# Attention of a graph network on one core: products and additions moved to GpSimd, one softmax for two chunks

## What is computed

```python
Q = (x @ Wq).reshape(N, H, D)      # N = 512, H = 8 heads, D = 32
K = (x @ Wk).reshape(N, H, D)
V = (x @ Wv).reshape(N, H, D)
score = jnp.einsum('nhd,ngd->nhg', Q, K) / np.sqrt(D)
score = jax.nn.softmax(score, axis=-1)
x1 = jnp.einsum('nhg,ngd->nhd', score, V).reshape(N, H * D)
msg = x1[dst] * x1[src]
attn_out = jax.ops.segment_sum(msg, dst, num_segments=N)
```

## Time and profile before

| | us |
|---|---|
| three runs before | 594.47, 595.21, 595.46 (median 595.21) |
| the profiled execution | 594.7 |
| its span | 592.6 |
| busy in it: TensorE, VectorE, ScalarE, GpSimd | 573.7, 462.4, 369.1, 224.1 |
| granted TensorE clock, mean | 0.999 |

### The profile page before, as it was taken

One profiled execution on the slowest core, in us unless ns is written; L12 is line 12 of the kernel. 1 busy time (PEld: TensorE's weight loads), 2 busy tenths in 40 slices (PEclk: granted clock), 3 DMA queues, 4 the chain that ended last, 5 costly groups with the idle time before them and its releaser, 6 DMA issues.

```text
span 592.6 us, 8599 instructions
## 1 busy us (share of the span) xinstructions
PE 573.7 (97%) x3032; PEld 487.7 (82%) x3032; DVE 462.4 (78%) x795; ACT 369.1 (62%) x565; POOL 224.1 (38%) x211
## 2 busy tenths in 40 slices
PE   7989999999999999999999999999999999898895
PEld 6778888888888888888888888888888889577763
DVE  5986497778878887788998789879766566798667
ACT  6866786777777766777766778757275543311242
POOL 4075577556666544554444555430000000000011
PEclk9999999999999999999999999999999999999999
DMA  8255487285576636546553875223182404000000
GB/s 295 79 205 175 143 288 218 106 285 172 170 223 189 215 106 214 160 155 212 178 192 128 319 239 164 91 81 91 46 317 74 152 0 143 0 2 0 1 0 35
DMA packets 34504, 86.86 MB, mean 147 GB/s; under 512 B 3872, under 2 KB 23200, under 8 KB 29856
## 3 DMA queue, kind: packets, MB, share of 16 engines
q1 hardware_dynamic: 27264, 67.09, 36.0%
q0 software_dynamic: 6912, 19.10, 8.5%
q10 hardware_dynamic: 288, 0.13, 0.1%
HBM read 66.69 MB, written 19.62 MB: 146 GB/s over the span
## 4 chain that ended last, share of the span: by engine, by line
PE 83%; DVE 10%; ACT 2%; issue 2%; POOL 1%; DMA 1%; POOLq 0%; DVEq 0%; ACTq 0%
PE ps L1337 27%; PE ps L1389 10%; PE ps L1543 7%; PE ps L1395 5%; PE ps L1371 5%; PE ps L1432 5%; PE ps L1367 4%; PE ps L1366 4%; PE ps L1507 4%; PE ps L1434 2%; PE ps L1585 2%; PE ps L1636 1%; PE ps L1555 1%; PE ps L1574 1%; PE ps L1351 1%
## 5 line engine op out<-in xcount | busy, mean ns | idle before, releaser
L483 POOL DMA_INDIRECT sorted_rows<-m,place x120 | 167.1, 1393 | 151.5 <-ACT m L546 123.5
L529 ACT ACTIVATE m_hi<-ps,cols 128x512 fp32r<-128x512 f32 x128 | 88.6, 692 | 67.0 <-PE ps L1337 41.5
L864 DVE TENSOR_TENSOR m_lo<-m_out,m_hi 128x512 fp32r<-128x512 f32 x128 | 88.5, 693 | 51.2 <-ACT m_out L531 48.2
L1337 PE MATMUL ps<-x_hi,w_hi 128*128 128x512 f32 x248 | 97.0, 391 | 0.5 <-DVE x_lo L738 0.5
L1337 PE MATMUL ps<-x_lo,w_hi 128*128 128x512 f32 x248 | 96.9, 391 | 0.0
L1337 PE MATMUL ps<-x_hi,w_lo 128*128 128x512 f32 x248 | 96.7, 390 | 0.0
L531 ACT ACTIVATE m_out<-ps,cols 128x512 f32<-128x512 f32 x128 | 88.5, 691 | 1.8 <-DVE m_lo L864 1.8
L738 DVE TENSOR_TENSOR x_lo<-x_raw,x_hi 128x1024 fp32r<-128x1024 f32 x62 | 73.1, 1218 | 5.3 <-ACT x_hi L523 5.3
L1389 PE MATMUL ps<-w_lo,m_hi 128*128 128x256 f32 x256 | 64.2, 283 | 0.0
L1389 PE MATMUL ps<-w_hi,m_hi 128*128 128x256 f32 x256 | 64.0, 282 | 0.0
L546 ACT ACTIVATE m<-m_in 128x512 f32<-128x512 f32 x64 | 39.5, 634 | 38.0 <-DVE m_in L877 38.0
(11 more groups left out here) (229 smaller groups left out, 1136.7 us busy)
## 6 DMA issues: line engine op xcount, KB each, us to landing
x_raw<-in_edges_dram SPq DMA_DIRECT2D x31, 1024.0 KB, 6.1
sorted_raw<-sorted_rows SPq DMA_DIRECT2D x24, 647.5 KB, 4.6
sorted_raw<-sorted_rows SPq DMA_DIRECT2D x6, 518.0 KB, 4.0
d_w<-in_d_dram SPq DMA_DIRECT2D x3, 1024.0 KB, 8.7
d_w<-in_d_dram SPq DMA_DIRECT2D x1, 3072.0 KB, 10.4
rows<-in_rows_dram SPq DMA_DIRECT2D x1, 2176.0 KB, 10.2
sorted_rows<-m,place POOLq DMA_INDIRECT x120, 4.8
w_raw<-in_w_dram SPq DMA_DIRECT2D x4, 256.0 KB, 5.4
```

What stands on the lines that cost most here:

```text
L483: pool.indirect_dma_start(out=sorted_d, out_offset=bass.IndirectOffsetOnAxis(ap=place[:, at:at + 1], axis=0), in_=m2[:, b % 2, t], in_offs ...
L529: nc.scalar.activation(out_hi[:, m], ps[:, bank], ACT.Gelu, bias=col(bias, m)).then_inc(hi_signal, 1)
L864: nc.vector.tensor_tensor(lo[:, m], m_out[:, m], hi[:, m].bitcast(F32), ALU.subtract).then_inc(done, 1)
L1337: last = nc.tensor.matmul(out, left, right, start=(k == 0 and i == 0), stop=(k == KE - 1 and i == 2))
```

## The change

The chunks' products are made and added in another split:

- GpSimd gets three instructions: `halves_of(0)` and `halves_of(1)` add the two halves (1024 elements each) of the output products 0 and 1; `last_scores(LOW_HEADS)` makes the half of score product 3 that belongs to heads 0 to 3 (1024 elements). VectorE makes the other half and no longer adds any halves; TensorE sums four parts of chunk 1 instead of eight.
- Score product 0 is made in two pieces of 1024 elements, the first ahead of the wait for the power and the normalized rows, and TensorE sums four parts after each piece.
- `less_top`, `exponential` and `softmax` take a range of chunks; chunks 2 and 3 go through them together, after the score reduction of chunk 3.
- TensorE's order becomes: `qkv(3)`, sum of scores 2, output sums 0 and 1, `gather(0)`, `gather(1)`, output sum 2, `gather(2)`, `gather(3)`. ScalarE's copies and exponentials follow it.

```diff
--- before.py
+++ after.py
@@ -280,6 +280,21 @@
 
             return ps[:, 2 + half, k * NH:(k + 1) * NH]
 
+        def last_scores(heads):
+
+            q = qk_rows[:, 3, 0:H].rearrange("p (h a d) -> p h a d", h=HEADS, a=1)
+            k = qk_rows[:, 3, H:2 * H].rearrange("p (a g d) -> p a g d", a=1, g=HEADS)
+            part = [P, heads.stop - heads.start, HEADS, DH]
+            out = prod[3].rearrange("p (h g d) -> p h g d", h=HEADS, g=HEADS)
+            return out[:, heads], q[:, heads].to_broadcast(part), k.to_broadcast(part), ALU.mult
+
+        LOW_HEADS, HIGH_HEADS = slice(0, HEADS // 2), slice(HEADS // 2, HEADS)
+
+        def halves_of(c):
+
+            half = HEADS * H // 2
+            return prod[c][:, 0:half], prod[c][:, 0:half], prod[c][:, half:], ALU.add
+
         def row_half(r):
 
             return r.rearrange("p (a f) -> p a f", a=1).to_broadcast([P, NC // 2, H])
@@ -330,6 +345,7 @@
         qkv_done, qkv_out = sem("qkv_done"), sem("qkv_out")
         scores_ready, exp_done = sem("scores_ready"), sem("exp_done")
         prod_ready, prod_summed = sem("prod_ready"), sem("prod_summed")
+        out_made, out_halved, scores_half = sem("out_made"), sem("out_halved"), sem("scores_half")
         x1_out, x1_ready, gathered = sem("x1_out"), sem("x1_ready"), sem("gathered")
         rz_weights = sem("rz_weights")
         wqk_ready, wv_ready = sem("wqk_ready"), sem("wv_ready")
@@ -503,6 +519,12 @@
             for half in range(2):
                 inverse_std(NODE_HALF[half])
                 inverse_std(NODE_HALF[half])
+            pool.wait_ge(out_made, 1)
+            pool.tensor_tensor(*halves_of(0)).then_inc(out_halved, 1)
+            pool.wait_ge(qkv_out, 2 * NC)
+            pool.tensor_tensor(*last_scores(LOW_HEADS)).then_inc(scores_half, 1)
+            pool.wait_ge(out_made, 2)
+            pool.tensor_tensor(*halves_of(1)).then_inc(out_halved, 1)
             for _ in ("o", "f2"):
                 for half in range(2):
                     inverse_std(NODE_HALF[half])
@@ -686,9 +708,9 @@
             nc.scalar.activation(wv_turned[:].rearrange("p k (d g) -> p k d g", g=HEADS),
                                  wv[:].rearrange("p k (g d) -> p k d g", g=HEADS), ACT.Copy).then_inc(wv_ready, 1)
 
-            def exponential(c, at):
+            def exponential(c, past, at):
                 act.wait_ge(scores_ready, at)
-                nc.scalar.activation(probs[:, c], probs[:, c], ACT.Exp, scale=float(DH) ** -0.5).then_inc(exp_done, 1)
+                nc.scalar.activation(probs[:, c:past], probs[:, c:past], ACT.Exp, scale=float(DH) ** -0.5).then_inc(exp_done, 1)
 
             def sums_out(c, at):
 
@@ -700,14 +722,13 @@
             qkv(0)
             qkv(1)
             affine(1, None, None)
-            exponential(0, 1)
-            exponential(1, 2)
+            exponential(0, 1, 1)
+            exponential(1, 2, 2)
             qkv(2)
             qkv(3)
-            sums_out(0, 3)
-            exponential(2, 3)
+            sums_out(0, 4)
+            exponential(2, 4, 3)
             sums_out(1, 5)
-            exponential(3, 4)
             sums_out(2, 6)
             for half in range(2):
                 affine(half, None, None)
@@ -1185,13 +1206,14 @@
             pairs = [P, HEADS, HEADS, DH]
             score_pairs = [P, DH, HEADS, HEADS]
 
-            def score_products(c):
+            def score_products(c, dims=slice(0, DH)):
+
                 dve.wait_ge(qkv_out, 2 * c + 1)
-                q = qk_rows[:, c, 0:H].rearrange("p (d h a) -> p d h a", h=HEADS, a=1).to_broadcast(score_pairs)
-                k = qk_rows[:, c, H:2 * H].rearrange("p (d a g) -> p d a g", a=1, g=HEADS).to_broadcast(score_pairs)
-
+                part = [P, dims.stop - dims.start, HEADS, HEADS]
+                q = qk_rows[:, c, 0:H].rearrange("p (d h a) -> p d h a", h=HEADS, a=1)[:, dims].to_broadcast(part)
+                k = qk_rows[:, c, H:2 * H].rearrange("p (d a g) -> p d a g", a=1, g=HEADS)[:, dims].to_broadcast(part)
                 view = prod[c].rearrange("p (d h g) -> p d h g", h=HEADS, g=HEADS)
-                return nc.vector.tensor_tensor(view, q, k, ALU.mult)
+                nc.vector.tensor_tensor(view[:, dims], q, k, ALU.mult).then_inc(prod_ready, 1)
 
             def scores(c, at):
 
@@ -1202,18 +1224,28 @@
             def each_g(t, c):
                 return t[:, c * HEADS:(c + 1) * HEADS].rearrange("p (r a) -> p r a", a=1).to_broadcast([P, HEADS, HEADS])
 
-            def less_top(c):
-
-                link(nc.vector.tensor_reduce(top[:, c * HEADS:(c + 1) * HEADS], probs[:, c], AX_X, ALU.max))
-                nc.vector.tensor_tensor(probs[:, c], probs[:, c], each_g(top, c), ALU.subtract).then_inc(scores_ready, 1)
-
-            def softmax(c, at):
+            def of_heads(t, c, past):
+
+                return t[:, c * HEADS:past * HEADS].rearrange("p (c h) -> p c h", h=HEADS)
+
+            def each_g(t, c, past):
+
+                one = t[:, c * HEADS:past * HEADS].rearrange("p (c h a) -> p c h a", h=HEADS, a=1)
+                return one.to_broadcast([P, past - c, HEADS, HEADS])
+
+            def less_top(c, past):
+
+                link(nc.vector.tensor_reduce(of_heads(top, c, past), probs[:, c:past], AX_X, ALU.max))
+                nc.vector.tensor_tensor(probs[:, c:past], probs[:, c:past], each_g(top, c, past),
+                                        ALU.subtract).then_inc(scores_ready, 1)
+
+            def softmax(c, past, at):
 
                 dve.wait_ge(exp_done, at)
-                one = slice(c * HEADS, (c + 1) * HEADS)
-                link(nc.vector.tensor_reduce(total[:, one], probs[:, c], AX_X, ALU.add))
+                one = slice(c * HEADS, past * HEADS)
+                link(nc.vector.tensor_reduce(of_heads(total, c, past), probs[:, c:past], AX_X, ALU.add))
                 link(nc.vector.reciprocal(total[:, one], total[:, one]))
-                link(nc.vector.tensor_tensor(probs[:, c], probs[:, c], each_g(total, c), ALU.mult))
+                link(nc.vector.tensor_tensor(probs[:, c:past], probs[:, c:past], each_g(total, c, past), ALU.mult))
 
             def out_products(c):
                 dve.wait_ge(qkv_out, 2 * c + 2)
@@ -1221,40 +1253,30 @@
                 v = v_rows[:, c].rearrange("p (g a d) -> p g a d", a=1, g=HEADS).to_broadcast(pairs)
                 return nc.vector.tensor_tensor(prod[c].rearrange("p (g h d) -> p g h d", h=HEADS, g=HEADS), sm, v, ALU.mult)
 
-            def halves_added(c, made):
-
-                dve.wait_ge(dve_step, made)
-                half = HEADS * H // 2
-                nc.vector.tensor_tensor(prod[c][:, 0:half], prod[c][:, 0:half], prod[c][:, half:],
-                                        ALU.add).then_inc(prod_ready, 1)
-
-
             dve.wait_ge(d2_done, NC)
-            moments(NODE_HALF[1])
-            score_products(0).then_inc(prod_ready, 1)
+            variance(NODE_HALF[1])
+            score_products(0, slice(0, DH // 2))
+            dve.wait_ge(rstd_ready, norms[0])
             hats_written(1, lambda c: normed(res, xp, c))
-            score_products(1).then_inc(prod_ready, 1)
+            score_products(0, slice(DH // 2, DH))
+            score_products(1)
             for c in range(2):
                 scores(c, c + 1)
-                less_top(c)
-                softmax(c, c + 1)
+                less_top(c, c + 1)
+                softmax(c, c + 1, c + 1)
                 if c == 0:
-                    out_made = step(out_products(c))
-            halves_added(0, out_made)
-            score_products(2).then_inc(prod_ready, 1)
-            out_products(1).then_inc(prod_ready, 1)
+                    out_products(0).then_inc(out_made, 1)
+            score_products(2)
+            out_products(1).then_inc(out_made, 1)
             dve.wait_ge(qkv_out, 2 * NC)
-            q = qk_rows[:, 3, 0:H].rearrange("p (h a d) -> p h a d", h=HEADS, a=1).to_broadcast(pairs)
-            k = qk_rows[:, 3, H:2 * H].rearrange("p (a g d) -> p a g d", a=1, g=HEADS).to_broadcast(pairs)
-            view = prod[3].rearrange("p (h g d) -> p h g d", h=HEADS, g=HEADS)
-            link(nc.vector.tensor_tensor(view, q, k, ALU.mult))
-            scores(2, 4)
-            less_top(2)
-            softmax(2, 3)
+            made = step(nc.vector.tensor_tensor(*last_scores(HIGH_HEADS)))
+            scores(2, 3)
+            dve.wait_ge(dve_step, made)
+            dve.wait_ge(scores_half, 1)
+            link(nc.vector.tensor_reduce(probs[:, 3], last_scores(slice(0, HEADS))[0], AX_X, ALU.add))
+            less_top(2, 4)
+            softmax(2, 4, 3)
             out_products(2).then_inc(prod_ready, 1)
-            link(nc.vector.tensor_reduce(probs[:, 3], view, AX_X, ALU.add))
-            less_top(3)
-            softmax(3, 4)
             sm = probs[:, 3].rearrange("p h (a g) -> p h a g", a=1).to_broadcast([P, HEADS, DH, HEADS])
```

(26 more changed lines are left out.)

## The result

The changed kernel takes 597.25 us (median of 22 executions, 594.82 to 598.11), the kernel before beside it 594.73 (22 executions, 594.07 to 595.46): ratio 1.0032, 95% interval 1.0024 to 1.0040. The medians lie 2.5 us apart; the ratio, 1.9 us, is what the means give (596.72 and 594.80), because the changed kernel's times fall into two groups and its median lies in the upper one. The forecast was 596.3, at the edge of what counts as slower.

What follows compares the result with a forecast made beforehand. VectorE's work and waits bound the stage before; afterwards TensorE, waiting for GpSimd, would. Terms -1.17, +1.84, -1.15, +2.25, -1.07 gave +0.70, then +1.14 through TensorE's path: 595.21 to 596.35 us, likeliest 596.3, range 592.3 to 597.8.

Steps and rivals of the forecast that it cites:

- The blocking: GpSimd's 1024-element instructions and VectorE's two-SBUF-input ones hold each other off; near 2.4 us each, +1.14 us, 34 in 100.
- the subtraction held off: VectorE's subtraction in `less_top(1)`, due at 520.37, waits for GpSimd's `halves_of(0)` until 522.21: +1.84 us.
- the second wait: VectorE's `out_products(1)`, or the next product, waits while GpSimd makes the low heads' half of score product 3: +2.25 us.
- the high heads' product: VectorE makes only this half of score product 3, saving 1.07 us; it ends at 531.37.
- The sum: All terms with blocking, to the end of the stage's last gather: 546.78 against 545.64, +1.14 us.
- the cold TensorE: TensorE's clock falls to 1.2 GHz after its 2.4 us standstill before chunk 1's output sum: up to +8.6 us, 3 in 100.
- The parts without conflict: Savings in the stage if engines did not disturb each other: gathers end at 542.8 against 545.64, 2.9 us faster.
- free sharing: Rival: GpSimd lets VectorE in between its reads, so VectorE's waits vanish: -2.9 us, 592.3 us, 15 in 100.
- one-sided blocking: Rival: only GpSimd is held up, VectorE not noticeably: -0.9 to +0.3 us, about 595 us, 15 in 100.
- A slow GpSimd: Rival: blocking with GpSimd's instructions over 2.42 us; 2.7 gives 597.3 us, 2.98 gives 598.1 us; 33 in 100.

Runs made afterwards that it cites:

- kernel 1: Changed kernel plus eight identity products whose result nobody reads, in TensorE's gap before the output sum of chunk 1: 595.36 us, ratio 1.0006.
- Kernel 2: Changed kernel with GpSimd's three instructions replaced by memsets of the same places, waits kept, its sums and products left out: 593.00 us, ratio 0.9968.
- kernel 8: Changed kernel with nothing but the powers on GpSimd; split score product 0, joint softmax and new TensorE order stay: 594.45 us, ratio 0.9990.
- kernel 9: Kernel before with score product 0 split and two one-input copies of 192 elements ahead of its first piece: 593.44 us, ratio 0.9972.
- kernels 5: Kernel before with only the addition of the halves of output product 0 moved to GpSimd: 595.48 us, ratio 1.0013.
- kernel 6: Kernel before with only the low heads' half of score product 3 moved to GpSimd: 595.94 us, ratio 1.0016.
- kernel 7: Kernel before with score product 0 split and one one-input copy of 192 elements ahead of its first piece: 594.39 us, ratio 0.9988.

## Why the prediction came out as it did

- **The blocking was right in mechanism, and 0.44 us too large in size.** Expected, then measured from the traces on one zero (after, less 1.10): `scores(0)` 515.42, 515.37; the subtraction held off by 1.84, 1.66; product 2 ends at 525.80, 525.53; the second wait 2.25, 2.14; the high heads' product ends at 531.37, 531.02; `halves_of(1)` ends at 533.64, 533.22. GpSimd needs 2.34 us for 1024 elements, not 2.4, which makes 0.18 of the 0.42 in three instructions. About half of the rest is that a held-off instruction of VectorE is nearly done at its release: the subtraction ends 0.09 us after it, where the sum put its whole 0.22 behind it. The sum was +1.14, without the clock it is +0.70 (kernel 1).
- **The step that failed is the cold TensorE.** The prediction found the 2.4 us gap (measured 2.34), gave its price as at most 8.6, and put it at 3 in 100, because nothing in the trace of before spoke for it. By the mean clocks it happened in 14 of 22 executions and in 2 of 3 later ones; both traced ones show it, and it cost 1.75 us in the first and 2.2 between the groups. The reading that the clock is not in play at gaps of 1.85 us rested on one execution: 6 of 81 later ones of the same kernel ran at a mean clock of 0.995, some 2 us longer. And for a gap of 2.34 it said nothing. That the work behind the gap was TensorE's alone, so that nothing would hide a slower clock, followed from the prediction's own sum and should have weighed more.
- **The parts without conflict were right.** Kernel 2, with the writes alone, shows -2.06 where free sharing was forecast as -2.9; of the 0.8 between, 0.58 is the wait for the power, held off here too, and most of the rest the rows of chunk 2 that come later for it. The joint softmax took 1.92 us from `less_top` to the next product (1.87 expected), and its cost behind it is shown by kernel 8.
- **The rivals.** Free sharing and one-sided blocking both fall: VectorE's own instructions are stretched by 1.66 and 2.14. The Trainium skill's rule ("SBUF — State Buffer", Who interferes with whom), that the two exclude each other for the whole instruction, agrees with these traces for 1024 elements too (4.43 in place of 2.29 us), and so does its exemption for reductions (2.29 at 532.49, beside GpSimd's reading) and for a GpSimd instruction that only writes (0.22 in kernel 2). Against it stands kernel 9: there the power of 0.79 us, though first by 0.16, doesn't hold the product off for its whole length, or at all. A slow GpSimd falls too: 2.34 us was measured for the addition of 1024 elements, and 2.36 for the product with repeated operands. The Trainium skill ("GPSIMD Engine Reference", Elementwise — side-by-side cycle accounting) has 4497 ns for one of 2048, and an estimate by half of that is 2.25 us, close to these traces.
- **That the total lies in the range is partly luck.** The errors differ in sign: blocking came out 0.44 us cheaper than the sum, the clock 1.75 to 2.2 dearer, and the median of before, which the forecast starts from, is 594.73 and not 595.21. From there the sum of +1.14 would give 595.9, and 597.25 was measured. The upper end of the range, 597.8, stood there for a slow GpSimd, and it took in a cost of the clock.

## What to carry to other kernels

Before work goes to GpSimd, list VectorE's instructions with two SBUF inputs that will run beside it: what is left of GpSimd's reading when such an instruction comes is added to VectorE, also for one of 64 elements (1.66 us of 2.34 here), so halving a product that way saved 1.07 us and cost 2.14. Place it where VectorE reduces or has one input, or let it only write. And where a new wait makes TensorE stand still as long as here (2.34 us) with its own work next on the path, reckon with the half clock behind it, or fill the gap with matmuls that nobody reads, as kernel 1 does.

## What the runs showed of the hardware

- The clock falls or doesn't for the same program: behind a gap of 2.34 us in 16 of 25 executions, 2 of them traced and the others told by their mean clock. The kernel before had times of 596.8 to 597.3 at a mean clock of 0.995 in 6 of 81 later executions, and kernels 5 and 6 of 597.4 to 598.1 at 0.994 or 0.995 in 3 of 12 each. These three share a gap of 1.85 us ahead of the first sum. In the traces of the other kernels no gap of the stage is longer than 1.20, because the split product takes the one of 1.85 away, and they had no time at 0.995 or less in 74 executions. That points to the gap of 1.85, but none of the executions at 0.995 of before, 5 and 6 was traced, and why the same gap is only sometimes enough stays open.
- In the one meeting of that kind (kernel 6) a waiting GpSimd got the turn ahead of VectorE's next instruction, although that was queued back to back; and of two that started in the same 10 ns VectorE's product won (once, kernel 7).
- The power of two elements holds VectorE's product off for 0.16 us at most: a product that starts so long after it takes its plain 1.22 us, and the power ends at 0.79 (kernel 9). When the power is the one held off, it ends 0.54 us after the release (0.69 undisturbed).
